# Opening of a windowed-attention and top-1 expert kernel: fewer warming products, another order of keys and queries, and two other engines for two of its steps

## What is computed

```python
x = x + attention(layernorm(x), W_qkv, b_qkv, W_out, b_out)   # softmax(q k^T / sqrt(8)), window 32
n = layernorm(x)
probs = softmax(n @ w_router)                                 # 8 columns; the best one, e
expert = (n @ w_up[e]) * silu(n @ w_gate[e]) @ w_down[e]      # for e < 7
shared = (n @ ws_up) * silu(n @ ws_gate) @ ws_down
out = x + 2 * probs[e] * expert + shared
```

## Time and profile before

| what | us |
|---|---|
| time, median of 3 (lowest, highest) | 345.61 (345.39, 347.31) |
| the profiled execution | 348.88 |
| its span | 347.2 |
| TensorE busy in it | 312.0 |
| VectorE | 217.9 |
| GpSimd | 188.2 |
| ScalarE | 149.0 |

### The profile page before, as it was taken

How to read it: one execution, slowest core, us unless ns; L and a number is a source line. 1 busy time by engine, 2 the same in 40 slices (tenths; PEclk the granted TensorE clock), 3 DMA queues, 4 the chain that set the end, 5 groups by cost and what they waited for, 6 DMA issues and landing times. The chain is left out here.

```text
span 347.2 us, 12270 instructions
## 1 busy us (share of the span) xinstructions
PE 312.0 (90%) x4914; PEld 253.2 (73%) x4914; DVE 217.9 (63%) x456; ACT 149.0 (43%) x267; POOL 188.2 (54%) x290
## 2 busy tenths in 40 slices
PE   8897989899799889995899999995999999999970
PEld 8755757576566656893878888784888888888860
DVE  6697889798799867889463333543555555555520
ACT  3344555434455644753132222332545545545420
POOL 7898558665469438594677544442333333333330
PEclk9999999999999989999899999998999999999996
DMA  7953142322414210895123211323333434333200
GB/s 198 351 128 77 60 120 47 96 51 83 101 43 120 59 46 2 320 344 145 41 70 110 94 62 64 61 62 53 76 74 66 74 63 75 72 77 75 66 16 0
DMA packets 53529, 32.49 MB, mean 94 GB/s; under 512 B 26448, under 2 KB 47700, under 8 KB 53474
## 3 DMA queue, kind: packets, MB, share of 16 engines
q1 hardware_dynamic: 48992, 23.18, 27.3%
q0 software_dynamic: 2880, 6.43, 5.3%
q10 hardware_dynamic: 1602, 2.10, 1.9%
HBM read 13.72 MB, written 11.95 MB: 74 GB/s over the span
## 5 line engine op out<-in xcount | busy, mean ns | idle before, releaser
L656 POOL DMA_INDIRECT out<-y,xn_base x38 | 37.3, 982 | 71.7 <-DVE y L1246 71.7
L1235 DVE TENSOR_TENSOR Pr<-psS,PT 128x512 f32<-128x512 f32 x38 | 26.3, 692 | 30.6 <-PE psS L1580 29.4
L1594 PE MATMUL psB<-down_sb,Pr 128*128 x304 | 40.4, 276 | 4.9 <-DVE y L1246 4.1
L1051 DVE TENSOR_TENSOR hT<-psS,PT 128x512 f32<-128x512 f32 x32 | 22.1, 691 | 33.1 <-PE psO L1484 25.8
L1594 PEld LDWEIGHTS psB<-down_sb,Pr 128*128 128x128 f32 x304 | 37.1, 192 | 5.4 <-issue 5.4
L818 ACT ACTIVATE PT<-psS 128x512 f32<-128x512 f32 x32 | 19.1, 597 | 51.0 <-PE psS L1472 40.6
L897 DVE TENSOR_REDUCE row_max<-psS 128x16 fp32r<-128x1024 f32 x32 | 37.6, 1215 | 2.4 <-PE psS L1319 2.4
L952 DVE STREAM_TRANSPOSE PT<-Pr 128x1024 f32<-128x1024 f32 x32 | 37.4, 1205 | 0.2 <-ACT Pr L740 0.2
L740 ACT ACTIVATE Pr<-psS 128x1024 f32<-128x1024 f32 x32 | 32.8, 1025 | 9.8 <-PE psS L1331 9.8
L860 ACT ACTIVATE PT<-psS 128x512 f32<-128x512 f32 x38 | 22.7, 597 | 27.2 <-PE psS L1574 27.2
L863 ACT COPY Pr<-psO 128x512 f32<-128x512 f32 x38 | 22.3, 587 | 22.2 <-PE psO L1586 22.2
(11 more groups left out here) (206 smaller groups left out, 701.9 us busy)
## 6 DMA issues: line engine op xcount, KB each, us to landing
sorted_rows<-pad_rows SPq DMA_DIRECT2D x9, 528.0 KB, 5.6
xn_base<-sorted_rows SPq DMA_DIRECT2D x38, 66.0 KB, 2.0
xs<-sorted_rows SPq DMA_DIRECT2D x152, 16.0 KB
rows<-in_L_attn_x SPq DMA_DIRECT2D x8, 256.0 KB, 6.0
VD_even<-V SPq DMA_DIRECT2D x28, 72.0 KB
VD_odd<-V SPq DMA_DIRECT2D x28, 72.0 KB, 2.4
gate_sb<-in_L_ffn_w_gate ACTq DMA_DIRECT2D x1, 1792.0 KB, 12.2
Kx<-K SPq DMA_DIRECT2D x28, 64.0 KB, 2.3
```

Source lines behind the costliest of these rows:

```text
L656: pool.indirect_dma_start(out=out_list, out_offset=bass.IndirectOffsetOnAxis(tok_u[:, r, :], 0), in_=y[:, r, :], in_offset=None, bounds_ch ...
L1235: nc.vector.tensor_tensor(hs[:, r % 2, :], psS[:, r % 2, 0:512], sg[:, r % 2, :], ALU.mult).then_inc(eh_done, 1)
L1594: last = mm(psB[:, 0:D], hsT[:, r % 2, c * P : (c + 1) * P], down_flat[:, bass.ds(start + c * D, D)], start=(c == 0), stop=(c == NC - 1),)
```

## The change

- TensorE: of the 48 warming products behind the bias product, 16 stay. Keys of batch 0 are made in two steps: tiles 0 and 1 first (signal `k_done`), then the queries, then tiles 2 and 3 (signal `late_k_done`). The wait for the late keys (`first_k_ready`) moves from scores of pair 0 to those of pair 1.
- The queries of batch 0 are evicted by VectorE, ahead of the late keys, and no longer by ScalarE.
- The half of `Kx[:, 1]` that VectorE cleared by a memset behind the values is cleared by ScalarE, early, by a multiplication with zero of the half that VectorE has cleared already. SyncE waits for it ahead of the key transfers of batch 1.
- VectorE takes the statistics of batch 2 behind the maximum of pair 0, ahead of those of batch 3.

```diff
 SyncE, spread_keys
                 if n == 1:
-                    sp.wait_ge(zeros_ready, 3)
+                    sp.wait_ge(zeros_ready, 2)
+                    sp.wait_ge(keys_cleared, 1)
 ScalarE, opening
+            act.wait_ge(zeros_ready, 2)
+            nc.scalar.activation(
+                Kx[:, 1, HPG // 2 :, :], Kx[:, 1, 0 : HPG // 2, :], ACT.Identity, bias=0.0, scale=0.0
+            ).then_inc(keys_cleared, 1)
             act.wait_ge(bqk_mm, 1)
...
             evict_k(0, 0)
-            evict_q(0, 0, first=True)
 VectorE, opening
-            dve.wait_ge(k_done, 1)
+            dve.wait_ge(q_done, 1)
+            nc.vector.tensor_scalar(Qx[:, 0, :], psA[:, :], bqk_sb[:, 0:1], None, ALU.add).then_inc(q_ready, 1)
+            dve.wait_ge(late_k_done, 1)
             dve.wait_ge(bk_of_ready, 1)
...
-            nc.vector.memset(Kx[:, 1, HPG // 2 :, :], 0.0).then_inc(zeros_ready, 1)
-            input_stats(2, stats1_done)
...
                 else:
+                    input_stats(2, stats1_done)
                     input_stats(3, stats1_done)
 TensorE
                     if b == 0:
                         pe.wait_ge(k_ready, 1)
-                        pe.wait_ge(first_k_ready, 1)
...
+                if p == 1:
+                    pe.wait_ge(first_k_ready, 1)
...
-            keep_warm(psS[:, 0, 0:P], 3 * WARM // 8)
+            keep_warm(psS[:, 0, 0:P], WARM // 8)
...
-            keys(0)
+            pe.wait_ge(xnT_ready, 1)
+            mm(psB[:, 0 : T // 2], wqk_sb[:, 1, :], xnT[:, 0 : T // 2], start=True, stop=True).then_inc(k_done, 1)
             queries(0)
+            mm(psO[:, 0, 0 : T // 2], wqk_sb[:, 1, :], xnT[:, T // 2 :], start=True, stop=True).then_inc(late_k_done, 1)
```

More of the change, by code:

```diff
@@ L218, in windowed_attention_top1_moe_kernel @@
         first_k_ready, first_v_ready = sem("first_k_ready"), sem("first_v_ready")
+        late_k_done, keys_cleared = sem("late_k_done"), sem("keys_cleared")
         norm_done, xt_done, xnT_ready = sem("norm_done"), sem("xt_done"), sem("xnT_ready")
@@ L1276, in keys @@
                 pe.wait_ge(xnT_ready, n + 1)
[L1277 to L1280, removed]
                 if n >= 2:
```

## The result

The changed kernel took 351.31 us (median of 4, 350.10 to 353.71) and the kernel before 345.73 beside it (345.39 to 347.31): a ratio of 1.016, 95% interval 1.012 to 1.021. It is slower by 5.6 us, where 1.1 less were forecast, and the range ended at 346.8. The same two kernels measured again, on another chip, gave 1.022 (1.015 to 1.029). Four of the seven executions of the changed kernel there lay over 1.5% above the quickest of them, and the median of the other three, 351.27, is 1.3% above the kernel before, so the size of the loss is known only as 1.3 to 2.2%. The profiled execution took 352.12 us, span 350.4, against 348.88 and 347.2. The traces of single executions therefore show only 3.2 us of the difference: that of the kernel before lies above its median.

The account below looks back on a forecast made before the run. The prediction took TensorE as busiest, held up by GpSimd's second chain and stops for instruction blocks. Opening -0.2 and instruction stream -0.9 made -1.1 us, the median going from 345.61 to 344.5, range 342.3 to 346.8.

Parts of the forecast that it names:

- Parts 1 to 6 of the opening: Opening through pair 0: earlier transposes, keys, queries and scores, ScalarE's clearing free; first maximum at 15.3, 1.95 us earlier.
- rival D: Opening fails: late weight or bias transfer, or 1.2 GHz clock at first real products; 344.7 or 345.6 us, chance 0.10.
- The cap at GpSimd: Transposes of batch 2 still wait for GpSimd until 28.89, so the opening brings only 0.2 us.
- The two steps ahead of it: Before batch 2's transposes: 0.5 us lost at batch 1's transposes, then pair 1 runs 1.4 us earlier.
- The stop of pair 2: TensorE's 1.11 us instruction stop ahead of batch 2's keys should go, as blocks end 64 instructions later in the program.
- The sum of the stops: TensorE's instruction stops in attention: eight blocks at 3.7 us each, 6.6 us of stops instead of 7.2, -0.6.
- Rival C: Slower: dense blocks end ahead of or among values in pairs 5, 9, 13, needing 4.1 us each; 348.0 us, chance 0.13.
- The upper bound of the term, +2.6: Worst case for TensorE's instruction stream in attention: blocks of 4.1 us, 9.8 us of stops, +2.6 us.
- The page that speaks of a hidden fetch: TensorE's instruction fetch is hidden behind issue, so removed instructions bring nothing; part of a rival at 345.4 us, chance 0.17.

Follow-up runs that it names:

- first group's run of the kernel before with 16 warming and 32 filled: Kernel before with 16 instead of 48 second warming products and 32 tiny useless products ahead of the transposes of batch 1: ratio 1.011.
- the run without the filling: Kernel before with 16 instead of 48 second warming products and nothing else: ratio 1.018.
- the second trace: Changed kernel, unchanged, measured and traced again on another chip: 353.82 us, ratio 1.022 to the kernel before.
- the second group: Changed kernel unchanged (1.022), with its first 64 warming products made 32 full and 64 half-size (1.003), or 128 half-size (1.011); kernel before repeated (0.998).
- the last run: Changed kernel with 96 first warming products, 20 full ones moved ahead of batch 1's transposes, and GpSimd's clearing later: 345.90 us, ratio 0.998 to the kernel before.

## Why the prediction was wrong, step by step

- **Parts 1 to 6 of the opening: right.** Transposes at 8.91 (8.98 said), ScalarE's keys 11.10 to 13.03 (11.15 to 13.08), VectorE's queries 0.75 (0.72 taken), scores of pair 0 at 13.17 (13.1 to 13.2), the first maximum at 14.94 (15.3). ScalarE's clearing ran in its idle time. The condition of rival D does occur: in the first group's run of the kernel before with 16 warming and 32 filled the granted clock was 0.50 from 10.8 us on, and the first maximum started at 17.19 instead of 15.93 in the run without the filling, which differs only behind it. In none of the twelve traces of the changed order did the clock fall before 18 us.
- **The cap at GpSimd: right**, shown by the second trace (1.71 us of waiting, transposes at 28.91) and by lifting it. The two steps ahead of it were too kind: 0.5 us were to be lost at the transposes of batch 1, and in seven of the twelve traces of the changed order the granted clock fell to 0.50, the 1.2 GHz level, right behind TensorE's idle time there (1.3 us in the first). This was named only under rival D and for the first products. It costs up to 1.6 us in pair 1 (start at 23.8 against 22.2), hidden by the cap in part; whether it is the rest of 1.003 is not shown.
- **The stop of pair 2: right.** No stop stands ahead of the keys of batch 2, and pair 2 lasted 7.1 us instead of 8.05.
- **The sum of the stops: wrong, and this is the step that failed.** "At 3.7 us for each they last 29.6: 6.6 us of stops instead of 7.2" counted only how much work a block holds and gave all blocks one length, which takes the delay of its transfer for fixed. The delay is what varies, by place: 0.6 to 2.5 us in the kernel before, up to 3.8 in the changed one. So the block of pair 4, with over 4 us of work, which the forecast passed over, stopped for 1.7, and those of pairs 8 and 12 for 1.4 and 1.2. The stops became 9.8 and 8.7 us in the traces of the stage, not 6.6, and the second group puts the cost of their place at 1.9% (1.022 against 1.003), 5.8 us between the medians. The spread stood in the trace of the kernel before: six of its 26 blocks had delays of 2.1 to 2.5 us, and by the count of instructions the blocks of pairs 6 and 14 lasted 3.9 and 4.6 us with their stops, where the prediction worked out 3.7 and 4.4.
- **Rival C was the case** by its sign and in part by its mechanism: the stops of pairs 5, 9 and 13 came, but the larger part came in pairs 4, 8 and 12. The point that it named, a transfer that starts over 2 us behind its block's first instruction, does not tell the kernels apart: six blocks of each had passed it; delays over 3 us are new. Its price, from 4.1 us a block, was less than half of what was measured: 348.0 against 351.3. The upper bound of the term, +2.6, should have been drawn from the longest block with its stop instead of a mean: an estimate with the 4.6 us of pair 14 is 8 x 4.6 - 23.0 = 13.8 us of stops, +6.6 and 352.0.
- **The page that speaks of a hidden fetch** (the Trainium skill, "Runtime: NRT & Kernel Launch", Instruction fetch mechanics) would have made the removed instructions worth nothing. The runs do not agree: 1.9% between two placements of the same work.
- The part of the 5.6 us that single traces do not show (they differ by 3.2) is not placed.

## What to carry to other kernels

Where an engine executes unrolled code faster than its blocks of instructions arrive, adding or removing instructions anywhere ahead shifts every later block end: before crediting an edit, run it once with the count of instructions held, with small ones put where they cost nothing and where they bring no late block into a stretch without slack, as the last run did. Read the stops for "issue" together with the instruction queue's transfers, block by block: one block's delay says little of the next one's. A train of DMA issues at that time is a suspect and not yet the cause; look for a late transfer with empty queues before blaming it. And a gain in an opening is worth only what the second chain, here GpSimd's, leaves of it.

## What the runs showed of the hardware

- A block's transfer of 16 KB started 0.6 to 2.5 us behind the block's first instruction in the attention stage of the kernel before, up to 3.8 us in the changed one, and 8.5 us in the opening of the last run; TensorE went on 2.3 to 2.8 us after the start where it had stopped. A delay of 3.1 us stands in a stretch in which no other transfer moved (133.2 to 138.7 us).
- With eight full value transfers for a batch the ratio is 1.016 and 1.022, with eight tiny ones 1.010, with one tiny one 1.002: the step from eight to one is just clear (1.004 to 1.017 against 0.998 to 1.005, on two chips), that from full to tiny is not.
- The same work behind 16, 32 or 64 small products more or less differs by up to 1.9% in time (1.022, 1.003 and 1.011 with 0, 64 and 128 half-size ones in the second group), and not in one direction only.
- The granted clock fell to 0.50 behind 1.3 us of idle TensorE in the opening in one execution and not in the next of the same kernel; with 20 warming products in the idle time it was 1.00 in the one trace taken, as in four of eleven without them.
